# Attention phase: the row transform, the weights and the inverse joined in one product with four matrices of the image

## The chip, the cores and the metric

The program runs on one core of a Trainium2 chip. The metric is device time in microseconds (us). The five engines are TensorE (PE; its weight loads are shown as PEld), VectorE (DVE), ScalarE (ACT), GpSimd (POOL) and SyncE (SP, which issues DMAs). PSUM is the memory into which TensorE writes its products; SBUF is the on-chip memory for everything else.

## The reference, cut to what matters

Thirty-two images of 256 x 256. A three-level Haar transform splits each into a low band and three times three detail bands. Each band is multiplied by a weight of the image (a sigmoid for the low band, three softmaxes for the details, of dot products over the whole image), and the inverse transform gives the rows back. A class row is put in front, then come a causal attention with a residual, and a layer of eight experts.

```python
for _ in range(3):
    cur, h, v, d = _dwt2(cur)             # Haar split of columns and rows
    details.append((h, v, d))
aw = sigmoid(cur.reshape(B, -1) @ Wa + ba)
rec = cur * aw[:, :, None]
for (h, v, d), (Wd, bd) in zip(reversed(details), det_params):
    w = softmax(stack([h, v, d]).reshape(B, -1) @ Wd + bd)
    rec = _idwt2(rec, h * w[:, 0], v * w[:, 1], d * w[:, 2])
h = concatenate([cls_tok, rec], axis=1)   # 257 rows of 256 per image
e = _layernorm(h)
h = h + softmax(e @ R @ e.T + causal) @ e
h = h + ffn(_layernorm(h))                # top-k rows of each of 8 experts
```

## The kernel before, in words

One image is two tiles (h = 0, 1) of 128 rows by 256 columns. The kernel has a start (the band weights are turned into an image, and 64 products give the logits of 16 images; the second half follows between the first steps), the attention phase, a search for each expert's threshold, and the expert phase.

The attention phase is a software pipeline with an order written out by hand. Every engine runs the same list of steps t = 0 to 35: steps 0 to 7 stand one by one, 8 to 27 are a hardware loop of five iterations with four steps each, the rest stand one by one again. In step t each engine works on five images: a = t, b = t-1, c = t-2, d = t-3, m = t-4. Semaphores carry the waits between engines; within an engine the order of the code holds. Of an image:

- GpSimd, one step ahead (`columns`, L457 to L464): the column transform into `Xc` by sums and differences in three levels, two instructions each.
- TensorE (a, L854): the row transform, `fwd` x `Xc`, 512 output columns into bank `Zb`.
- VectorE (a): `Zb` times the table `W8` (L1279, two instructions), then the inverse column transform in three levels (L1284 to L1297) into `Q`.
- TensorE (b, L839): the inverse row transform `inv` x `Q` into bank `Hb`.
- VectorE (b): mean and variance of `Hb` (L1258, L1264). ScalarE (b): a copy of `Hb` into `hc` (L650).
- GpSimd (`emit`, L487 to L497): reciprocal deviations by a power (L492) and the scales that follow, for both layer norms at once: of b (input of attention) and of m (its output). It waits for the statistics of both. Behind them come `columns` of the next image and small copies into tables (L500, L472, L478).
- ScalarE (b, L663): the normalised rows `Ex`. TensorE (c, L847): their transpose; ScalarE (L641) copies it to `ET`. TensorE (c, L874): the product with R, 1024 columns; ScalarE (L656) copies it to `GT`. TensorE (c, L894, L896): the scores with the causal mask. VectorE (c, L1321, L1325): gate terms and row maxima.
- ScalarE (d, L634, L636): the exponentials. TensorE (d, L866): their transposes; ScalarE (L646) copies them. TensorE (d, L884 to L886): times the rows. VectorE (d): `U` (L1306), `H1` with the residual (L1314), its statistics (L1331, L1337). ScalarE writes `Yp` (m, L671) and `Bs` (one image older, L614), and SyncE stores both.

TensorE's order in a step is L839 (b), L847 (c), L854 (a), L866 (d), L874 (c), L884 to L886 (d), L894 and L896 (c). VectorE's is the first statistics (b), the inverse transform (a), `U` and `H1` (d), maxima (c), second statistics (d). ScalarE's is exponentials (d), `ET` (c), copy of transposes (d), `hc` (b), `Bs`, `GT` (c), `Ex` (b), `Yp` (m).

## Time and profile before

| what | value |
|---|---|
| median of 3 runs (lowest, highest) | 832.46 us (831.77, 833.66) |
| the profiled execution, its own time | 832.74 us |
| its span in the profile | 829.2 us |
| busy share of the span: PE, DVE, ACT, POOL | 89%, 70%, 55%, 56% |
| start, up to the first `fwd` product | 0 to 46.8 us |
| attention phase, up to the last `Bs` | about 46.8 to 329.6 us |
| threshold search, placing, first gathers | about 330 to 399 us |
| expert phase | about 399 to 829 us |

The page gives the busy time of each engine, the span in 40 slices, the DMA queues and the chain of work that ended last. Its busy shares are means over four phases with different limits, so the attention phase has to be read from windows and timelines of its own. In the rows below, a start time is that of the first of the instructions merged into the row (x2 is two instructions), the second number is their time from first start to last end, and a bracket at the end is the engine's idle time before them with what released it.

### The profile page before, as it was taken

How to read it: one execution, taken by the hardware profiler on the slowest of the kernel's cores; microseconds unless marked ns; L12 is line 12 of the kernel's file. 1: busy time of each engine (PE TensorE's matmuls, PEld its weight loads, DVE VectorE, ACT ScalarE, POOL GpSimd, SP SyncE). 2: the span in 40 equal slices, each digit the busy share in tenths (PEclk: the TensorE clock that was granted, in tenths of full speed). 3: DMA queues.
4: the chain of work that ended last, by engine and by line, in shares of the span. 5: the costliest groups of instructions: out<-in, count | busy, mean ns of one | idle time of the engine just before them, and what ended most of it. 6: DMA issues, size and time to landing. Idle time of an engine off the chain costs nothing.

```text
span 829.2 us, 15989 instructions
## 1 busy us (share of the span) xinstructions
PE 742.1 (89%) x4566; PEld 640.6 (77%) x4566; DVE 577.6 (70%) x1968; ACT 454.2 (55%) x1001; POOL 464.9 (56%) x744
## 2 busy tenths in 40 slices
PE   6988999999999984872799999999989999999994
PEld 3976667667667663761699998999989989999994
DVE  3765888888888876998878476684765856644431
ACT  1012677777777775200556665556655666566551
POOL 0155677777677755403426648467484673855533
PEclk9989999999999998555899999999999999999997
DMA  9900022122122122701213424334243352433222
GB/s 268 292 3 2 30 77 77 51 76 76 51 76 74 54 77 96 158 21 40 71 26 75 113 41 128 69 69 122 40 121 67 52 146 39 103 84 54 40 24 27
DMA packets 63570, 64.43 MB, mean 78 GB/s; under 512 B 14033, under 2 KB 57105, under 8 KB 63377
## 3 DMA queue, kind: packets, MB, share of 16 engines
q1 hardware_dynamic: 50576, 46.57, 18.7%
q0 software_dynamic: 12800, 17.12, 12.8%
q8 instruction: 26, 0.43, 0.2%
q14 instruction: 40, 0.32, 0.1%
q10 hardware_dynamic: 128, 0.00, 0.0%
HBM read 38.14 MB, written 25.53 MB: 77 GB/s over the span
## 4 chain that ended last, share of the span: by engine, by line
PE 33%; DVE 9%; issue 8%; POOL 5%; ACT 3%; DMA 2%; POOLq 0%; ACTq 0%; DVEq 0%; SPq 0%
PE bank L959 14%; PE bank L973 14%; PE bank L948 2%; DMA raw<-in_fc1T 2%; POOL w2l L517 2%; PE bank L985 1%; POOL out L553 1%; POOL yg L531 1%; ACT bank L706 1%; DVE Tc L1389 1%; DVE yl L1508 1%; DVE jk L1485 1%; PE bank L938 1%; DVE TR L1373 1%; DMA yg<-rows,idx 1%
## 5 line engine op out<-in xcount | busy, mean ns | idle before, releaser
L553 POOL DMA_INDIRECT out<-ob,sidx x72 | 114.0, 1583 | 159.4 <-ACT ob L722 145.7
L1515 DVE TENSOR_TENSOR hl<-bank,hh 128x384 fp32r<-128x384 f32 (+1 forms) x192 | 97.5, 513 | 138.5 <-ACT hh L709 134.8
L706 ACT ACTIVATE bank<-bank,b1s 128x384 f32<-128x384 f32 (+1 forms) x192 | 99.5, 518 | 137.7 <-PE bank L959 132.5
L959 PE MATMUL bank<-yh,w1h 128*128 128x384 f32 (+1 forms) x384 | 132.6, 345 | 9.5 <-DVE hl L1515 6.4
L959 PE MATMUL bank<-yh,w1l 128*128 128x384 f32 (+1 forms) x384 | 123.4, 321 | 0.0
L959 PE MATMUL bank<-yl,w1h 128*128 128x384 f32 (+1 forms) x384 | 122.9, 320 | 0.0
L973 PE MATMUL bank<-w2l,hh 128*128 128x256 f32 x384 | 108.0, 281 | 0.0
L973 PE MATMUL bank<-w2h,hh 128*128 128x256 f32 x384 | 108.0, 281 | 0.0
L973 PE MATMUL bank<-w2h,hl 128*128 128x256 f32 x384 | 107.9, 281 | 0.0
L531 POOL DMA_INDIRECT yg<-rows,idx x72 | 72.4, 1006 | 55.7 <-issue 50.6
L709 ACT ACTIVATE hh<-bank 128x384 fp32r<-128x384 f32 (+1 forms) x192 | 87.7, 457 | 6.1
L959 PEld LDWEIGHTS bank<-yh,w1h 128*128 128x128 f32 x384 | 73.8, 192 | 14.6 <-DVE hl L1515 7.8
L959 PEld LDWEIGHTS bank<-yl,w1h 128*128 128x128 f32 x384 | 73.5, 191 | 0.0
L959 PEld LDWEIGHTS bank<-yh,w1l 128*128 128x128 f32 x384 | 72.8, 190 | 0.0
L973 PEld LDWEIGHTS bank<-w2l,hh 128*128 128x128 f32 x384 | 72.6, 189 | 0.0
L973 PEld LDWEIGHTS bank<-w2h,hh 128*128 128x128 f32 x384 | 72.5, 189 | 0.0
L973 PEld LDWEIGHTS bank<-w2h,hl 128*128 128x128 f32 x384 | 72.5, 189 | 0.0
L874 PE MATMUL bank<-ET,Rw 128*128 128x256 f32 x256 | 62.4, 386 | 0.0
L874 PEld LDWEIGHTS bank<-ET,Rw 128*128 128x128 f32 x256 | 46.0, 189 | 9.7 <-issue 3.3
L894 PE MATMUL bank<-GT,ET 128*128 128x137 f32 (+1 forms) x256 | 52.5, 340 | 0.7 <-ACT GT L656 0.7
L492 POOL TENSOR_TENSOR ST<-A,mhalf 128x6 f32<-128x6 f32 x36 | 50.7, 1408 | 3.0
L663 ACT ACTIVATE ARENA<-bank,N,ST 128x256 f32<-128x256 f32 x64 | 32.6, 560 | 33.0 <-POOL O L497 33.0
(224 smaller groups left out, 1815.5 us busy)
## 6 DMA issues: line engine op xcount, KB each, us to landing
BIG<-in_x SPq DMA_DIRECT2D x4, 2048.0 KB, 16.4
out<-Bs SPq DMA_DIRECT2D x32, 256.0 KB, 2.2
rows<-Yp SPq DMA_DIRECT2D x32, 256.0 KB, 2.4
raw<-in_fc1T SPq DMA_DIRECT2D x16, 512.0 KB
raw<-in_fc2T SPq DMA_DIRECT2D x16, 512.0 KB
yg<-rows,idx POOLq DMA_INDIRECT x72, 2.9
out<-ob,sidx POOLq DMA_INDIRECT x72, 3.8
gwb<-in_gate_w SPq DMA_DIRECT2D x1, 1024.0 KB, 7.2
```

What stands on the lines that cost most here:

```text
L492: g.tensor_tensor(st[:, 8:14], A6[:, :], mhalf[:, :], ALU.pow).then_inc(s["pow"], 1)
L517: rest = g.tensor_tensor(flat(lo, half), raw[:, half * NF:(half + 1) * NF], flat(hi, half), ALU.subtract)
L531: g.indirect_dma_start(out=yg[eh][0:m, t, :], out_offset=None, in_=rows, in_offset=tok(ap=idx[eh][0:m, t:t + 1], axis=0))\
L553: g.indirect_dma_start(out=out_rows, out_offset=tok(ap=sidx[job.eh][0:m, t:t + 1], axis=0), in_=ob[t % 3][0:m, :], in_offset=None, compute ...
L663: last = A.activation(Ex[b.r][:, h, 0:D], Hb[:, h * D:(h + 1) * D], ACT.Identity, bias=N6[t.p][:, h:h + 1], scale=ST[t.p][:, 8 + h:9 + h])
L706: A.activation(h[:, 0:cur.w], h[:, 0:cur.w], ACT.Gelu_apprx_tanh, bias=b1s[:, bass.ds(cur.e, 1), f]).then_inc(s["hact"], 1)
L709: A.activation(hT[cur.p][0][:, f, 0:cur.w], h[:, 0:cur.w], ACT.Copy).then_inc(s["hhi"], 1)
L874: last = T.matmul(Rb[:, e * D:(e + 1) * D], Rw[:, j, e * P:(e + 1) * P], ET[c.p][:, j, 1:NT], start=(j == 0), stop=(j == 1))
L894: T.matmul(Sb[:, c0:c0 + w], ET[c.p][:, j, 1 + h * P:1 + (h + 1) * P], GT[c.p][:, j, 0:w], start=(j == 0), stop=False)
L959: last = T.matmul(Lb[ring(cur, f)][:, 0:cur.w], w1s[cur.eh][i][:, d, f * P:(f + 1) * P], yT[cur.p][k][:, d, 0:cur.w], start=(n == 0), stop ...
L973: mm = T.matmul(bank[4 + t % 2][:, 0:D], hT[prev.p][i][:, f, at:at + P], w2s[prev.eh][k][:, f, :], start=(n == 0), stop=(n == 23))
L1515: v.tensor_tensor(hT[cur.p][1][:, f, 0:cur.w], Lb[ring(cur, f)][:, 0:cur.w], hT[cur.p][0][:, f, 0:cur.w], ALU.subtract).then_inc(s["hlo"], 1)
```

## The change

The row transform, the multiplication by the weights and the inverse row transform of an image are all linear maps on its 128 rows, and a Haar transform of three levels mixes only rows within blocks of 8. So for each of the four column bands (`LEAF` = 4) there is one matrix `inv` x diag(weights) x `fwd`, with the same 8 x 8 block sixteen times on its diagonal. The change builds these blocks once per half of the images into a table `OB` (128 x 32 images x 32): VectorE expands the weights (`mix_blocks`), TensorE folds them with one product of 512 columns (`fold`), ScalarE copies the product to `OB` (`mix_table`). In each step GpSimd spreads the blocks of the next image into the four 128 x 128 matrices `OP` (`operators`: one multiplication by a mask, 512 elements per partition). TensorE makes four products with them in place of the two before, 640 output columns in place of 1024. The column transform stops at two levels: the pair for the third (L463, L464) goes, and the last product reads its columns in exchanged pairs instead.

VectorE no longer multiplies by the table. It copies the low band (128 elements) and makes the last two levels of the inverse column transform straight from PSUM into `hc`, then takes the first statistics from `hc`, all for image a in step t and not for b. ScalarE's copy into `hc` goes, and `Ex` is made from `hc`. TensorE's and ScalarE's other instructions keep their order. In step 3 TensorE waits for the logits' mask and not for the table.

```diff
-for _name, _n in [("ident", P), ("fwd", P), ("inv", P), ("same", P), ("before", P), ("causal", P),
-                  ("sign", 3), ("slot", 9), ("batch", 1), ("diag", CG), ("pick", NJ), ("spread", 4 * P),
+for _name, _n in [("ident", P), ("same", P), ("before", P), ("causal", P),
+                  ("sign", 3), ("slot", 9), ("batch", 1), ("diag", CG), ("pick", NJ), ("fold", P), ("mixed", 4 * CG), ("blocks", P),
                   ("owner", 5), ("rep1", P), ("rep2", P), ("rep3", 2 * P), ("halves", 2 * BITS)]:
...
-                po.wait_ge(s["xc_l"], m.n * 2 + 1)
-                g.tensor_tensor(L2[:, :, :], L1[:, :, 0::2], L1[:, :, 1::2], ALU.add).then_inc(s["xc_l"], 1)
-                g.tensor_tensor(dst[:, :, 64:128], L1[:, :, 0::2], L1[:, :, 1::2], ALU.subtract)
-                po.wait_ge(s["xc_l"], m.n * 2 + 2)
-                g.tensor_tensor(dst[:, :, 0:32], L2[:, :, 0::2], L2[:, :, 1::2], ALU.add)
-                g.tensor_tensor(dst[:, :, 32:64], L2[:, :, 0::2], L2[:, :, 1::2], ALU.subtract).then_inc(s["xc"], 1)
+                po.wait_ge(s["xc_l"], m.n + 1)
+                g.tensor_tensor(dst[:, :, 0:64], L1[:, :, 0::2], L1[:, :, 1::2], ALU.add)
+                g.tensor_tensor(dst[:, :, 64:128], L1[:, :, 0::2], L1[:, :, 1::2], ALU.subtract).then_inc(s["xc"], 1)
+
+            def operators(m):
+
+                after(po, "z_done", m.n - 1)
+                apart(po)
+                blocks = OB[:, bass.ds(m.n, 1), :].rearrange("p b (g k) -> p (b g) k", g=LEAF)
+                g.tensor_tensor(OP[m.p].rearrange("p g (r k) -> p g r k", k=CG),
+                                blocks.unsqueeze(2).to_broadcast([P, LEAF, P // CG, CG]),
+                                cst("blocks").rearrange("p (r k) -> p r k", k=CG).unsqueeze(1)
+                                .to_broadcast([P, LEAF, P // CG, CG]), ALU.mult).then_inc(s["wide"], 1)
...
                     columns(nxt)
+                    if isinstance(t.n, int) and t.n == HEAD - 1:
+                        po.wait_ge(s["w8"], 2)
+                    operators(nxt)
...
             columns(Step(0, 0))
+            po.wait_ge(s["w8"], 1)
+            operators(Step(0, 0))
...
+            def mix_table(i):
+
+                act.wait_ge(s["w8_mm"], i + 1)
+                A.activation(OB[:, i * HB:(i + 1) * HB, :].rearrange("p b k -> p (b k)"), ZP[:, :], ACT.Copy)\
+                    .then_inc(s["w8"], 1)
+            mix_table(0)
...
-                if b:
-                    after(act, "h1", b.n - 3)
-                    act.wait_ge(s["st0_b"], b.n + 1)
-                    A.activation(hc[b.r][:, :, :], Hb[:, :].rearrange("p (h c) -> p h c", h=NH), ACT.Copy)
...
-                        last = A.activation(Ex[b.r][:, h, 0:D], Hb[:, h * D:(h + 1) * D], ACT.Identity,
+                        last = A.activation(Ex[b.r][:, h, 0:D], hc[b.r][:, h, :], ACT.Identity,
...
+                T.matmul(ZP[:, :], cst("fold")[0:CG * NJ, :], bw8[:, :, :].rearrange("p b k -> p (b k)"),
+                         start=True, stop=True).then_inc(s["w8_mm"], 1)
...
-                    after(pe, "hcE", b.n)
-                    pe.wait_ge(s["q"], b.n + 1)
-                    T.matmul(Hb[:, :], cst("inv"), Q[b.p].rearrange("p h c -> p (h c)"), start=True, stop=True)\
-                        .then_inc(s["h0"], 1)
...
-                    after(pe, "zw", a.n * 2)
+                    after(pe, "q", a.n)
+                    pe.wait_ge(s["wide"], a.n + 1)
                     pe.wait_ge(s["xc"], a.n + 1)
-                    T.matmul(Zb[:, :], cst("fwd"), Xc[a.p].rearrange("p h c -> p (h c)"), start=True, stop=True)\
-                        .then_inc(s["z_done"], 1)
+                    X, Z = Xc[a.p], Zb[:, :].rearrange("p (h c) -> p h c", h=NH)
+                    T.matmul(Z[:, :, 128:256], OP[a.p][:, 3, :], X[:, :, 128:256], start=True, stop=True)
+                    T.matmul(Z[:, :, 64:128], OP[a.p][:, 2, :], X[:, :, 64:128], start=True, stop=True)
+
+                    T.matmul(Z[:, :, 0:64], OP[a.p][:, 0, :], X[:, :, 0:64], start=True, stop=False)
+                    T.matmul(Z[:, :, 0:64].rearrange("p h (c s) -> p h c s", s=2), OP[a.p][:, 1, :],
+                             X[:, :, 0:64].rearrange("p h (c s) -> p h c s", s=2)[:, :, :, ::-1],
+                             start=False, stop=True).then_inc(s["z_done"], 1)
...
-                    pe.wait_ge(s["w8"], 2)
+                    pe.wait_ge(s["lg_m"], 2)
...
+            def mix_blocks(i):
 
                 dve.wait_ge(s["z_mm"], 2 * i + 2)
-                v.tensor_copy(bwT[:, i * HB:(i + 1) * HB], ZP[i][0:NJ, 32:32 + HB]).then_inc(s["bw_c"], 1)
-
-            def mix_table(i):
-
-                dve.wait_ge(s["w8_mm"], i + 1)
-                for q, (c0, c1) in enumerate(((0, 1), (1, 2), (2, 4), (4, 8))):
-                    last = v.tensor_copy(W8[:, i * HB:(i + 1) * HB, c0:c1],
-                                         ZP[i][:, 128 + q * HB:128 + (q + 1) * HB].unsqueeze(2)
-                                         .to_broadcast([P, HB, c1 - c0]))
-                last.then_inc(s["w8"], 1)
+                after(dve, "w8_mm", i)
+                v.tensor_tensor(bw8[:, :, :], ZP[0:CG * NJ, 32:32 + HB].unsqueeze(2).to_broadcast([CG * NJ, HB, LEAF * CG]),
+                                cst("mixed")[0:CG * NJ, :].unsqueeze(1).to_broadcast([CG * NJ, HB, LEAF * CG]), ALU.mult)\
+                    .then_inc(s["bw_c"], 1)
...
+                if a:
+
+                    dve.wait_ge(s["z_done"], a.n + 1)
+                    Z = Zb[:, :].rearrange("p (h c) -> p h c", h=NH)
+                    v.tensor_copy(I2[:, :, :], Z[:, :, 0:64]).then_inc(s["i4"], 1)
+                    dve.wait_ge(s["i4"], a.n + 1)
+                    v.tensor_tensor(I1[:, :, 0::2], I2[:, :, :], Z[:, :, 64:128], ALU.add)
+                    v.tensor_tensor(I1[:, :, 1::2], I2[:, :, :], Z[:, :, 64:128], ALU.subtract).then_inc(s["inv"], 1)
+                    dve.wait_ge(s["inv"], a.n + 1)
+                    v.tensor_tensor(hc[a.r][:, :, 0::2], I1[:, :, :], Z[:, :, 128:256], ALU.add)
+                    v.tensor_tensor(hc[a.r][:, :, 1::2], I1[:, :, :], Z[:, :, 128:256], ALU.subtract).then_inc(s["q"], 1)
+                    dve.wait_ge(s["q"], a.n + 1)
                     for h in range(NH):
-                        last = v.bn_stats(bn0[:, h, :], Hb[:, h * D:(h + 1) * D])
+                        last = v.bn_stats(bn0[:, h, :], hc[a.r][:, h, :])
                     last.then_inc(s["st0_b"], 1)
-                if b:
-                    dve.wait_ge(s["st0_b"], b.n + 1)
+
+                    after(dve, "tab", t.n)
+                    dve.wait_ge(s["st0_b"], a.n + 1)
                     apart(dve)
                     for h in range(NH):
-                        last = v.bn_aggr(st[:, 2 * h:2 + 2 * h], bn0[:, h, :])
+                        last = v.bn_aggr(ST[1 - t.p][:, 2 * h:2 + 2 * h], bn0[:, h, :])
...
-                    for g0, g1 in ((0, 2), (2, 8)):
-                        w = W8[:, bass.ds(a.n, 1), g0:g1].to_broadcast([P, NH, g1 - g0]).unsqueeze(3)\
-                            .to_broadcast([P, NH, g1 - g0, 32])
-                        v.tensor_tensor(Zw.rearrange("p h (g c) -> p h g c", g=8)[:, :, g0:g1, :],
-                                        Zb[:, :].rearrange("p (h g c) -> p h g c", h=NH, g=8)[:, :, g0:g1, :], w,
-                                        ALU.mult).then_inc(s["zw"], 1)
-                    dve.wait_ge(s["zw"], a.n * 2 + 1)
-                    lo, hi = Zw[:, :, 0:32], Zw[:, :, 32:64]
-                    v.tensor_tensor(I2[:, :, 0::2], lo, hi, ALU.add)
-                    v.tensor_tensor(I2[:, :, 1::2], lo, hi, ALU.subtract).then_inc(s["inv"], 1)
-                    dve.wait_ge(s["zw"], a.n * 2 + 2)
-                    dve.wait_ge(s["inv"], a.n * 2 + 1)
-                    hi = Zw[:, :, 64:128]
-                    v.tensor_tensor(I1[:, :, 0::2], I2[:, :, :], hi, ALU.add)
-                    v.tensor_tensor(I1[:, :, 1::2], I2[:, :, :], hi, ALU.subtract).then_inc(s["inv"], 1)
-
-                if a:
-                    dve.wait_ge(s["inv"], a.n * 2 + 2)
-                    after(dve, "h0", a.n - 1)
-                    hi = Zw[:, :, 128:256]
-                    v.tensor_tensor(Q[a.p][:, :, 0::2], I1[:, :, :], hi, ALU.add)
-                    v.tensor_tensor(Q[a.p][:, :, 1::2], I1[:, :, :], hi, ALU.subtract).then_inc(s["q"], 1)
...
+            row = haar[p, 0:CG]
+            mixed[j, :, g, :] += (1 / 8, 1 / 8, 1 / 4, 1 / 2)[g] * scale[p] * np.outer(row, row)
+    mixed[:, :, 0, :], mixed[:, :, 1, :] = mixed[:, :, 0, :] + mixed[:, :, 1, :], mixed[:, :, 0, :] - mixed[:, :, 1, :]
+    put("mixed", mixed.reshape(NJ * CG, LEAF * CG))
+    put("fold", m[:, None] % CG == q[None, :] % CG)
+    put("blocks", q[:, None] // CG == q[None, :] // CG)
```

GpSimd, step 7, the last one ahead of the loop, from the scales of the step to the table copy. Before (`Xc` and `L1` lie in ARENA, the image in BIG):

```order
L495 TENSOR_TENSOR N<-ST,nm 128x4
L496 TENSOR_TENSOR N<-ST,nm 128x2
L497 TENSOR_SCALAR O<-ST 128x2
L457 TENSOR_TENSOR ARENA<-BIG 128x256
L458 TENSOR_TENSOR ARENA<-BIG 128x2x128
L460 TENSOR_TENSOR ARENA<-ARENA 128x128
L461 TENSOR_TENSOR ARENA<-ARENA 128x2x64
L463 TENSOR_TENSOR ARENA<-ARENA 128x2x32
L464 TENSOR_TENSOR ARENA<-ARENA 128x2x32
L500 COPY TST<-ST 128x16
```

GpSimd at the same place now (`OP` lies in ARENA too, the mask in C):

```order
L503 TENSOR_TENSOR N<-ST,nm 128x4
L504 TENSOR_TENSOR N<-ST,nm 128x2
L505 TENSOR_SCALAR O<-ST 128x2
L458 TENSOR_TENSOR ARENA<-BIG 128x256
L459 TENSOR_TENSOR ARENA<-BIG 128x2x128
L461 TENSOR_TENSOR ARENA<-ARENA 128x2x64
L462 TENSOR_TENSOR ARENA<-ARENA 128x2x64
L469 TENSOR_TENSOR ARENA<-OB,C 128x512
L511 COPY TST<-ST 128x16
```

The pair with 64 outputs is gone, and one instruction with 512 stands in its place, ahead of the table copy.

VectorE, step 7, from the first statistics to `U`. Before:

```order
L1258 BN_STATS bn<-bank 128x6 x2
L1264 BN_AGGR ST<-bn 128x2 x2
L1272 RECIPROCAL ST<-rsm 128x2
L1279 TENSOR_TENSOR ARENA<-bank,W 128x2x64
L1279 TENSOR_TENSOR ARENA<-bank,W 128x2x192
L1284 TENSOR_TENSOR ARENA<-ARENA 128x64
L1285 TENSOR_TENSOR ARENA<-ARENA 128x64
L1289 TENSOR_TENSOR ARENA<-ARENA 128x128
L1290 TENSOR_TENSOR ARENA<-ARENA 128x128
L1296 TENSOR_TENSOR ARENA<-ARENA 128x256
L1297 TENSOR_TENSOR ARENA<-ARENA 128x256
L1306 SCALAR_TENSOR_TENSOR ARENA<-CX,ARENA,bank 128x264 x2
```

VectorE at the same place now:

```order
L1283 COPY ARENA<-bank 128x128
L1285 TENSOR_TENSOR ARENA<-ARENA,bank 128x128
L1286 TENSOR_TENSOR ARENA<-ARENA,bank 128x128
L1288 TENSOR_TENSOR hc<-ARENA,bank 128x256
L1289 TENSOR_TENSOR hc<-ARENA,bank 128x256
L1292 BN_STATS bn<-hc 128x6 x2
L1299 BN_AGGR ST<-bn 128x2 x2
L1305 RECIPROCAL ST<-rsm 128x2
L1313 SCALAR_TENSOR_TENSOR ARENA<-CX,ARENA,bank 128x264 x2
```

The first statistics moved behind the inverse transform, and they are now those of the step's own image.

TensorE, step 7, from the inverse to the product with R (Rw). Before:

```order
L839 MATMUL bank<-ARENA,C 128x512
L847 MATMUL bank<-C,ARENA 128x128 x4
L854 MATMUL bank<-ARENA,C 128x512
L866 MATMUL bank<-C,ARENA 128x128 x3
L874 MATMUL bank<-ET,Rw 128x256 x4
```

TensorE at the same place now:

```order
L870 MATMUL bank<-C,ARENA 128x128 x4
L879 MATMUL bank<-ARENA 128x2x128
L880 MATMUL bank<-ARENA 128x2x64
L882 MATMUL bank<-ARENA 128x2x64
L883 MATMUL bank<-ARENA 128x2x64
L896 MATMUL bank<-C,ARENA 128x128 x3
L855 MATMUL bank<-ET,Rw 128x256 x4
```

The inverse (L839) is gone, so the transposes of c come first, and four products stand where `fwd` stood.

## Rows read from the trace of the kernel before

**Rows 1.** Windows: busy us (instructions) of each engine, granted TensorE clock, DMA share, GB/s.
```profile
200.00:300.00 100.00, 98.06 (x451) 69.33 (x449) 87.38 (x310) 74.77 (x179) 73.28 (x207) 1.00 0.19 65
```

**Rows 2.** Timeline of one step: start us, us, engine, line, tiles, [idle <-releaser].
```profile
202.63 1.97 PE L874 MATMUL bank<-ET,Rw 128*128 128x256 f32 x8
...
204.43 0.61 PE L884 MATMUL bank<-ARENA 128*128 128x264 f32 x2
...
205.97 0.89 DVE L1306 SCALAR_TENSOR_TENSOR ARENA<-CX,ARENA,bank 128x264 f32<-128x264 f32 x2 [0.47 <-PE bank L886]
...
206.95 1.03 DVE L1314 SCALAR_TENSOR_TENSOR H<-ARENA,ST,hc 128x256 f32<-128x256 f32 x2
...
207.99 0.61 DVE L1325 TENSOR_REDUCE nmx<-bank 128x1 f32<-128x129 f32 x2
...
208.64 0.37 ACT L634 ACTIVATE ARENA<-bank,nmx 128x129 f32<-128x129 f32 x1 [0.58 <-DVE nmx L1325]
...
209.36 0.25 DVE L1337 BATCH_NORM_AGGREGATE ST<-bn 128x2 f32<-128x6 f32 x2
209.44 0.60 ACT L641 ACTIVATE ET<-bank 128x512 f32<-128x512 f32 x1
...
210.19 1.97 PE L874 MATMUL bank<-ET,Rw 128*128 128x256 f32 x8
```

**Rows 3.** Timelines: key product early and late, one stall, two H1 updates.
```profile
90.88 0.30 PEld L839 LDWEIGHTS bank<-ARENA,C 128*128 128x128 f32 x2 [1.68 <-ACT ARENA L663]
...
93.90 1.90 PE L874 MATMUL bank<-ET,Rw 128*128 128x256 f32 x8
...
292.79 1.26 DVE L1314 SCALAR_TENSOR_TENSOR H<-ARENA,ST,hc 128x256 f32<-128x256 f32 x2
...
300.65 0.88 DVE L1314 SCALAR_TENSOR_TENSOR H<-ARENA,ST,hc 128x256 f32<-128x256 f32 x2
...
303.81 1.97 PE L874 MATMUL bank<-ET,Rw 128*128 128x256 f32 x8
...
311.30 1.97 PE L874 MATMUL bank<-ET,Rw 128*128 128x256 f32 x8
```

**Rows 4.** Timeline of the same step: GpSimd and the first product.
```profile
202.72 0.25 DVE L1264 BATCH_NORM_AGGREGATE ST<-bn 128x2 f32<-128x6 f32 x2
...
203.12 0.22 POOL L487 TENSOR_SCALAR A<-ST 128x4 f32<-128x4 f32 x1 [1.60 <-DVE ST L1264]
...
204.73 0.43 DVE L1296 TENSOR_TENSOR ARENA<-ARENA 128x256 f32<-128x256 f32 x1
...
205.98 0.61 POOL L457 TENSOR_TENSOR ARENA<-BIG 128x256 f32 x1
...
208.21 0.29 POOL L463 TENSOR_TENSOR ARENA<-ARENA 128x64 f32<-128x64 f32 x1
...
208.80 1.13 PE L854 MATMUL bank<-ARENA,C 128*128 128x512 f32 x2
```

**Rows 5.** Timeline at the end of one loop iteration.
```profile
178.79 0.76 DVE L1258 BATCH_NORM_STATS2 bn<-bank 128x6 f32<-128x256 f32 x2 [0.36 <-issue]
...
184.21 1.12 PE L839 MATMUL bank<-ARENA,C 128*128 128x512 f32 x2 [0.38 <-ACT ARENA L663]
```

**Rows 6.** Groups of instructions by form, GpSimd: x count | busy us, mean ns | idle.
```profile
L517 POOL TENSOR_TENSOR w2l<-raw,w2h 128x1024 fp32r<-128x1024 f32 x16 | 38.4, 2401 | 5.2 <-ACT w2h L685 4.9
...
L460 POOL TENSOR_TENSOR ARENA<-ARENA 128x128 f32<-128x128 f32 x32 | 17.3, 540 | 0.0
```

**Rows 7.** DMA issues of the start: KB each, us to landing.
```profile
C<-in_const SPq DMA_DIRECT2D x1, 940.0 KB, 4.9
```

**Rows 8.** Timeline of the start and the first steps.
```profile
7.68 15.41 PE L759 MATMUL bank<-ARENA,C 64*128 64x384 f32 x40 [7.68 <-DMA ARENA<-in_Wd]
...
46.78 2.05 PE L854 MATMUL bank<-ARENA,C 128*128 128x512 f32 x2
...
61.45 1.10 PE L854 MATMUL bank<-ARENA,C 128*128 128x512 f32 x2
```

103 lines of the change are left out of this document (50 added, 53 removed).

## The prediction

> **What bounds the kernel now.** I read the windows first, since the page's shares are means over four phases and the change touches the start and the attention phase alone. In the attention phase TensorE is busy 98.06 us of 100, VectorE 87.38, ScalarE 74.77, GpSimd 73.28, at full clock [rows 1]. That invites the reading that TensorE sets the pace and that every column taken from it comes back as time. The timelines say otherwise, so I followed one step by its starts.
>
> The attention chain of a step [rows 2]: the product with R starts at 202.63; 1.80 us later the products of the probabilities (204.43); 1.54 later `U` (205.97), for which VectorE had sat idle 0.47; 0.98 to `H1` (206.95); 1.04 to the maxima (207.99); 0.65 to the exponentials (208.64), before which ScalarE was idle 0.58; 0.80 to the copy `ET` (209.44), which stands behind the exponentials in ScalarE's order; 0.75 to the next product with R (210.19). Sum 7.56 us, the whole step. The chain closes on itself: each R product stands ahead of the next image's probabilities on TensorE, and the next `ET` behind that image's exponentials on ScalarE. The change touches no link of it. A better witness is at the end of the phase: from 303.81 to 311.30 [rows 3] the loop has run out of images, there is no first product, no inverse, no column transform and no weights, and the step still takes 7.49 us.
>
> A second chain runs through GpSimd and takes two steps [rows 4]. First statistics end at 202.97 (202.72 + 0.25), GpSimd starts 0.15 later, 2.86 later (205.98) it begins the columns, and the first product starts when they are done, at 208.80; then 1.39 to the R product of rows 2.
>
> A third shows at the loop's end [rows 5]: VectorE takes the first statistics 0.36 us late at 178.79, and the inverse product, which needs the `Ex` made from them, starts at 184.21 after an idle 0.38 with ScalarE's `Ex` as releaser. Between the R starts at 93.90 and 303.81 [rows 3] lie 27 steps in 209.91 us, 7.774 each, against 7.56 for the good one: such late steps make the mean.
>
> **The change part by part.**
>
> *TensorE.* 1024 columns become 640. R's 1024 columns take 1.80 us [rows 2], 1.76 ns each, so 384 fewer are 0.68 us per step, off a busy time of 98.06% of 7.774, or 7.62. TensorE falls to about 6.95. By the chain of rows 2 this is worth nothing directly: R starts when `ET` is there. What it buys is slack ahead of R. The inverse goes with its wait for `Ex`; the transposes take that wait over.
>
> *VectorE.* In place of eight instructions on SBUF and the table, and of statistics from PSUM, there are a copy, four sums and the same statistics. None of the five has more outputs than the 256 of L1296, 0.43 us [rows 4], though one operand now lies in PSUM: at most 2.15. Statistics of this kind and their join took from the maxima's end (207.99 + 0.61) to 209.61, 1.0 us [rows 2]. The first products will end some 1.35 us after their start; the start was 208.80, so 210.15, and `U` is due at 205.97 + 7.56 = 213.53. At most 3.15 us of work fits into the 3.38 between them. So nothing of it shows, with 0.2 to 0.8 of slack; if the sums from PSUM took 0.55 each, `U` would be 0.4 late in every step. The statistics are now ready a step ahead of GpSimd's need.
>
> *ScalarE.* The copy of `Hb` goes, about 0.6 us like the `ET` copy of the same size [rows 2]. It was behind the exponentials and `ET`, so it is off the chain and worth nothing.
>
> *GpSimd.* It loses the pair from 208.21 to the product's start at 208.80, 0.59 us [rows 4], and gains one multiplication of 512 elements. No row of before has these operands (two inputs, one repeated over rows, the other over matrices). The nearest in length is the subtraction of 1024 in 2401 ns, 2.34 ns each [rows 6]: 1.20 us. The dearest is L460 at 540 ns for 128 outputs, 4.22 ns each [rows 6]: 2.16 us. The cheapest is L457 at 0.61 for 256 [rows 4], no less. I take 1.20, with 0.10 for the start and the hand-over, because the added one reads and writes in runs of eight neighbours while L460 reads every second element. Bounds: 1.1 and 2.3.
>
> Now the two-step chain with the new wait (`wide`), which every image's first product has. GpSimd starts when the second statistics end, at 209.61 in rows 2, and no longer after the first ones. Hand-over 0.15; to the columns 2.86; four column instructions 2.23 (205.98 to 208.21); multiplication 1.30; first products and transposes 1.39 plus 128 columns more, 0.22: 1.61; R to probabilities 1.80; to `U` 1.54; `U` to the end of the second statistics 3.64 (205.97 to 209.61). Sum 15.13 for two steps, 7.57 each. Behind the waiting product on TensorE stand the transposes of the probabilities, R and all else, so a late GpSimd would delay the whole step. GpSimd's own load: 73.28% of 7.774 is 5.70, minus 0.59 plus 1.30, 6.41 us: it fits.
>
> The Trainium skill ("GPSIMD Engine Reference", Performance versus the Vector engine) puts two-input elementwise work at about 2.6 cycles of 1.2 GHz per element. By it the multiplication would take an estimated 1.11 us and the chain 7.53 a step; the row's 2.34 ns is a little above, so the sum stays with the row.
>
> So both chains ask for 7.56 to 7.57. The late steps should mostly go: the 0.36 of VectorE at the loop's end falls into its slack, and `Ex` comes 0.9 us earlier, since GpSimd starts after the second statistics (209.61, a step earlier 202.05) and no longer after the first (202.97). I leave 0.1 for each of the five ends, which makes 7.6 a step with the jitter of rows 2, and 0.5 beside it. Gain: 209.91 - 27 x 7.6 = 4.7, less 0.5: 4.2.
>
> *The start.* The constants shrink from 1880 to 1400 columns, 940 to 700 KB. Their DMA took 4.9 us [rows 7], and the first products wait at 7.68 for a transfer behind it on the same queue [rows 8]. 240/940 of 4.9 is 1.25, an upper bound since part of it is latency; I take 0.8 earlier, for all that follows. Against that, the first product of image 0 (46.78) now waits for the table: a product of 512 columns in place of eight small ones, ScalarE's copy (0.6) in place of VectorE's, and GpSimd's multiplication (1.3). The last two are 1.9 us, of which I take half as covered by the class row's products; 128 columns more cost 0.5 there, where 512 took 2.05 and not the 1.10 of the same product at 61.45 [rows 8]. That is 1.5 later. In step 5 the inverse's weights sat 1.68 us waiting for `Ex` [rows 3]; that wait goes with GpSimd's earlier start, and I take 1.2 of it. Net 0.5 earlier; bounds 2.0 earlier (0.8 + 1.2, the table's path all covered) and 2.0 later (1.9 + 0.5 and nothing gained in step 5, less 0.4 for the constants).
>
> *After the phase* nothing is changed; the last steps without first products keep their 7.49.
>
> Sum against the profiled execution: 832.74 - 4.2 - 0.5 = 828.0. The median shown is 832.46, 0.28 below that execution; a difference this small is below what can be told, so 828.0 stands.
>
> **The rivals.**
>
> *B, GpSimd becomes the bound (slower).* If the multiplication takes L460's 4.22 ns per element, its term is 2.26 instead of 1.30, the two-step chain 16.09, 8.05 a step. 27 x (8.05 - 7.774) = 7.5 more, and the start some 0.5 later instead of earlier: 840.7. It decides from a chain of 15.55, that is, from a multiplication of about 1.7 us. For it: twelve instructions of GpSimd now stand between the second statistics and the first product, and the sum has no slack. Against: L457 and the 1024-element row both say 2.3 to 2.4 ns, the former with reads of every second element as well.
>
> *C, `H1` is slowed in each step.* The two `H1` instructions take 1.26 us beside column instructions, 1.03 in the good step, 0.88 beside nothing [rows 2, 3]. They lie on the attention chain. Now GpSimd works from 3.0 to 6.5 us after the second statistics on columns and multiplication, and `H1` starts 4.9 after them (206.95 + 7.56 - 209.61). If the multiplication slows both halves like the worst columns do, the chain is 7.56 + 0.23 = 7.79 or, from 7.49 + 0.38, 7.87; I take 7.83. 27 x 0.06 = 1.5 more, less 0.5: 833.7. The Trainium skill ("GPSIMD Engine Reference", Key points) says that GpSimd contends for its SBUF interfaces with VectorE instructions that have two SBUF inputs. `H1` is such a one, and the three durations agree. By that rule the second half of `H1` would be slowed by the multiplication, as the first is by the last column instruction.
>
> *D, the long steps stay.* They come from the branch itself and not from the statistics' way to `Ex`. Then the step keeps 7.774 and only the start counts: 832.2. Against it: the releaser in rows 5 is `Ex`.
>
> *E, more comes back.* If `H1` falls between GpSimd's instructions that do no harm, the attention chain is 7.49: 27 x 0.284 = 7.7 and 0.5 from the start: 824.5.
>
> **How the numbers follow.** Forecast 0.50 (825.5 to 830.7, from a multiplication of 1.1 to 1.4 and the start's bounds), B 0.15, C 0.15, D 0.10, E 0.10. The range 824.0 to 834.5 leaves out B and about a twentieth more, the far ends of E and C. This kernel's measurement tells 0.2% from no change, 1.7 us, so faster means below 830.8 and slower above 834.1. Faster: 0.48 of the forecast, E 0.10, C 0.04, D 0.02, 0.64. Same: C 0.08, D 0.07, 0.02 of the forecast, 0.17. Slower: B 0.15, C 0.03, D 0.01, 0.19.
>
> **What would show it.** The R product's starts should lie 7.5 to 7.65 apart, without a long one at each loop's end; TensorE should be idle some 0.5 us a step ahead of the R product or the transposes, released by ScalarE, and its busy share of the window should fall to about 91%; VectorE should still wait for the probabilities ahead of `U`. The multiplication's mean should be 1.15 to 1.35. The first products of TensorE should start at 7.68 - 0.8, and the gap between R's starts at the step numbers of 93.90 and 303.81 should be near 205.7. I am wrong if the first product waits for the multiplication by more than 0.3 us in most steps (B), if `H1` is 1.2 us or more throughout (C), or if VectorE starts `U` later than the probabilities allow because its new sums run late.

## The result: slower by 3.4%

The changed kernel takes 860.68 us (median of 4 runs, 858.98 to 862.99) against 832.12 us (4 runs, 831.29 to 833.66): ratio 1.034, 95% interval 1.0318 to 1.0362. Forecast were 828.0 us and a range of 824.0 to 834.5. The profiled execution took 860.9 us, its span 859.1; before these were 832.74 and 829.2.

Where the 29.9 us of span lie, by the starts of four instructions:

| from, to | before | after | difference |
|---|---|---|---|
| start to the R product of the step at 93.90 [rows 3] | 93.90 | 95.15 | +1.25 |
| 27 steps from there | 209.91 (7.774 each) | 229.93 (8.516 each) | +20.02 |
| from there to the first placing product | 76.18 | 77.48 | +1.30 |
| from there to the end | 449.21 | 456.54 | +7.33 |

The attention phase again, windows of the changed kernel, columns as in [rows 1]. TensorE's busy share fell to 83 where 91 was forecast, and every other engine but GpSimd fell too: a new wait, not new work.

```profile
200.00:300.00 100.00, 82.89 (x457) 67.90 (x456) 80.51 (x244) 64.05 (x153) 73.93 (x175) 1.00 0.18 63
```

The attention chain of one step, to be laid beside [rows 2]: timeline of the changed kernel (start us, us, engine, line, tiles, idle and releaser).

```profile
202.09 1.96 DVE L1321 SCALAR_TENSOR_TENSOR H<-ARENA,ST,hc 128x256 f32<-128x256 f32 x2
202.09 1.27 POOL L469 TENSOR_TENSOR ARENA<-OB,C 128x512 f32<-128x512 f32 x1
...
203.42 0.70 PE L879 MATMUL bank<-ARENA 128*128 128x256 f32 x2 [0.38 <-POOL ARENA L469]
203.97 0.16 DVE L1328 COPY ARENA<-bank 128x16 f32<-128x16 f32 x1
204.05 0.61 DVE L1332 TENSOR_REDUCE nmx<-bank 128x1 f32<-128x129 f32 x2
...
204.77 0.37 ACT L655 ACTIVATE ARENA<-bank,nmx 128x129 f32<-128x129 f32 x1 [2.39 <-DVE nmx L1332]
...
205.58 0.59 ACT L663 ACTIVATE ET<-bank 128x512 f32<-128x512 f32 x1
...
205.83 0.52 PE L896 MATMUL bank<-C,ARENA 128*128 128x128 f32 x3 [1.05 <-ACT ARENA L657]
...
206.32 1.97 PE L855 MATMUL bank<-ET,Rw 128*128 128x256 f32 x8
...
208.13 0.61 PE L911 MATMUL bank<-ARENA 128*128 128x264 f32 x2
...
209.66 0.89 DVE L1313 SCALAR_TENSOR_TENSOR ARENA<-CX,ARENA,bank 128x264 f32<-128x264 f32 x2 [1.33 <-PE bank L913]
```

`H1` (L1321) and GpSimd's multiplication (L469) start in the same hundredth of a microsecond, and `H1` takes 1.96 us for 1.03 [rows 2] or 0.88 [rows 3]. All links behind it keep their lengths to 0.07 us; ScalarE waits 2.39 us for the maxima (0.58 before). One step is 8.55 us, 7.49 + 1.06, and this repeats in each step that has a multiplication. The multiplication starts 6.6 us after the end of the previous `H1` (204.05 to 210.64), by way of the second statistics. `H1` starts, by way of the exponentials, after just as long (the next one stands at 210.64 too), and so they meet again.

The expert part lost 7.3 us, though its code is unchanged. TensorE's waits there, by releaser (us in total, times, longest), in the changed kernel; the kernel before has no wait for issue at this line:

```profile
PE bank L986 <- issue: 8.0, 2, 4.0
```

They lie at 628 to 637 us, where the expert loop's first pass (experts 1 and 5) ends and the program jumps back for the second. The windows there, columns as above, show 16 us with TensorE half busy (8.0 us), and the granted clock at its lower level (0.50, 1.2 GHz) behind the idle time:

```profile
628.00:632.00 4.00, 0.61 (x6) 0.40 (x4) 3.82 (x9) 1.23 (x3) 3.70 (x3) 0.84 0.48 73
632.00:636.00 4.00, 0.68 (x1) 0.50 (x2) 1.70 (x3) 0.00 (x0) 3.67 (x3) 0.50 0.74 187
636.00:640.00 4.00, 2.71 (x11) 2.70 (x11) 0.00 (x0) 0.73 (x2) 3.14 (x3) 0.50 0.44 124
640.00:644.00 4.00, 4.00 (x27) 4.00 (x27) 1.04 (x2) 1.88 (x4) 0.00 (x0) 0.88 0.29 100
```

The queue that brings instructions moved more, too. Its row in the list of DMA queues (packets, MB, share), before and then after:

```profile
q8 instruction: 26, 0.43, 0.2%
```
```profile
q8 instruction: 36, 0.59, 0.3%
```

### The profile page after: what moved, and what is told of

It reads as the page before. It is cut to its first block, busy times and chain, and to the rows that moved or that the text cites. A ratio compares the mean times of both kernels' runs of the same rounds, so it can differ in the third digit from the quotient of the medians.

```text
span 859.1 us, 15856 instructions
## 1 busy us (share of the span) xinstructions
PE 728.0 (85%) x4684; PEld 655.1 (76%) x4684; DVE 578.3 (67%) x1870; ACT 443.3 (52%) x971; POOL 483.6 (56%) x712
## 4 chain that ended last, share of the span: by engine, by line
PE 32%; DVE 9%; issue 8%; POOL 5%; ACT 3%; DMA 2%; POOLq 0%; ACTq 0%; DVEq 0%; SPq 0%
PE bank L986 14%; PE bank L1000 13%; PE bank L1012 2%; PE bank L975 2%; POOL out L566 2%; POOL w2l L530 2%; POOL yg L544 1%; DMA raw<-in_fc1T 1%; ACT bank L727 1%; DVE Tc L1396 1%; DVE yl L1515 1%; DVE jk L1492 1%; PE bank L965 1%; DVE TR L1380 1%; DVE ohu L1467 1%
## 5 line engine op out<-in xcount | busy, mean ns | idle before, releaser
L1321 DVE SCALAR_TENSOR_TENSOR H<-ARENA,ST,hc 128x256 f32<-128x256 f32 x64 | 57.6, 938 | 2.8
L1313 DVE SCALAR_TENSOR_TENSOR ARENA<-CX,ARENA,bank 128x264 f32<-128x264 f32 x64 | 28.4, 485 | 42.6 <-PE bank L913 42.6
```

What stands on the lines that cost most here:

```text
L1313: last = v.scalar_tensor_tensor(out=U[d.p][:, h, :], in0=CX[:, :], scalar=Pr[d.p][:, 129 * h:129 * h + 1], in1=Ab[h][:, 0:DG], op0=ALU.mul ...
L1321: last = v.scalar_tensor_tensor(out=H1[d.p][:, h, :], in0=U[d.p][:, h, 0:D], scalar=st_next[:, 14 + h:15 + h], in1=hc[d.r][:, h, :], op0=A ...
```

## The experiments

Two causes were in question: who holds `H1`, and what stalls the expert loop. Ratios are to the kernel before the change, run on the same chip.

### What holds H1

**The multiplication moved.** In `emit` of GpSimd, from behind `columns` to behind the two table copies, with its wait for the second half of the table:

```
+                if nxt:
+                    if isinstance(t.n, int) and t.n == HEAD - 1:
+                        po.wait_ge(s["w8"], 2)
+                    operators(nxt)
                 if b:
                     after(po, "hcE", b.n - 1)
...
                 if nxt:
                     columns(nxt)
-                    if isinstance(t.n, int) and t.n == HEAD - 1:
-                        po.wait_ge(s["w8"], 2)
-                    operators(nxt)
```

> GpSimd's multiplication (128x512, 1.27 us) is issued 2 us later in the program: behind its two table copies of the next step and ahead of its statistics, where it has idled 1.2 us for combine1's result in the changed kernel. Nothing is left out. Theory (a GpSimd instruction that is running when H1 is ready holds H1 until it ends, and nothing else went wrong): H1 meets at most the last column instruction (0.40 us), so it takes 0.9 to 1.3 us for 1.95, the statistics start up to 0.3 us later, the distance from one R product to the next falls from 8.55 to 7.5 to 7.9 us, and the kernel takes 860.7 - 31 x (0.65 to 1.05) = 828 to 841 us. Rival 1 (the product of each image is late because the multiplication ends late: TensorE waited 0.37 us per step for it): gains at most 0.37 x 31 = 11 us, 849, and H1 stays at 1.95. Rival 2 (VectorE's five sums that read PSUM are what lengthened the step): nothing changes, 861.

Measured 832.32 us, ratio 0.9998 (0.9988 to 1.0008): 28 us came back by moving one instruction. The timeline of one step:

```profile
202.99 0.89 DVE L1314 SCALAR_TENSOR_TENSOR ARENA<-CX,ARENA,bank 128x264 f32<-128x264 f32 x2 [1.32 <-PE bank L914]
...
203.74 0.40 POOL L462 TENSOR_TENSOR ARENA<-ARENA 128x128 f32<-128x128 f32 x1
203.96 0.88 DVE L1322 SCALAR_TENSOR_TENSOR H<-ARENA,ST,hc 128x256 f32<-128x256 f32 x2
204.09 0.42 POOL L512 COPY TST<-ST 128x16 f32 x1
204.76 0.17 DVE L1329 COPY ARENA<-bank 128x16 f32<-128x16 f32 x1
...
205.58 1.27 POOL L469 TENSOR_TENSOR ARENA<-OB,C 128x512 f32<-128x512 f32 x1
```

The multiplication still takes 1.27 us, but `H1` 0.88 (0.88 to 1.03 in the attention loop); the R products lie 7.4 to 7.6 us apart. Rivals 1 and 2 are out: the wait of 0.38 for L469 couldn't give 28 us, and the sums from PSUM are unchanged. The expert part kept its loss: the first placing product is at 375.87 us (379.99 before), the span 832.3 (829.2).

**Half of the multiplication.** `gs = slice(0, 2)` for the matrices from the third image on; the other two matrices keep old values.

> From the third step on GpSimd's multiplication makes two of the four matrices (256 elements in each partition for 512); the other two keep what an earlier step left in them, so this leaves out half of the weights' work. Place and count of the instruction are the changed kernel's. Theory (held for the rest of the running instruction): the multiplication takes 0.65 us for 1.27 and H1 1.30 to 1.40 for 1.95; the step is 8.55 - 0.6 = 7.95 us and the kernel 860.7 - 30 x 0.6 = 843 us. Rival (contention as two streams sharing a rate): H1 overlaps only 0.65 us of traffic at half speed, so it takes 0.88 + 0.33 = 1.2 us, the step 7.8 and the kernel 838. Rival (the sums that read PSUM): 861.

Measured 845.71 us, ratio 1.0162 (1.0134 to 1.0191).

**A copy in its place.** It leaves out the mask.

```
-                g.tensor_tensor(OP[m.p]..., blocks..., cst("blocks")..., ALU.mult)
+                g.tensor_copy(OP[m.p].rearrange("p g (r k) -> p g r k", k=CG),
+                              blocks.unsqueeze(2).to_broadcast([P, LEAF, P // CG, CG]))
```

> The multiplication is a copy of the same 512 elements at the same place: one input, the table of blocks repeated over the columns; the mask is left out, so the matrices aren't block-diagonal. Theory in its narrow form (only two two-input instructions from SBUF shut each other out): H1 is back at 0.88 us, the step at 7.5 and the kernel at 860.7 - 31 x 1.05 = 828 us. Theory in its wide form (any GpSimd instruction holds H1 while it runs): a copy of 512 elements takes at least 0.4 us, so H1 takes 0.88 plus the copy's duration and the step 7.49 plus it. The duration of H1 beside the copy tells the two apart. Rival (the sums that read PSUM): 861.

Measured 841.56 us, ratio 1.0092 (1.0064 to 1.012). The narrow form is out: an instruction with one input holds `H1` as well.

**H1 with one input in PSUM.** `in1=Ab[h][:, 0:D]` for `in1=hc[d.r][:, h, :]`, and TensorE's `after(pe, "u", d.n)` becomes `after(pe, "h1", d.n)`. It leaves out the residual.

> H1's second input is the product in PSUM (128x256 of the bank that U has just read) for hc in SBUF, so H1 reads one input from SBUF and one from PSUM; the residual is left out of H1. TensorE's AV of the next step waits for H1 for U, which comes 0.9 us earlier and is not late. GpSimd is as in the changed kernel. Theory (H1 is held because both its inputs are in SBUF): H1 takes 0.9 us though the multiplication of 1.27 us runs beside it, the step is 7.5 us and the kernel 860.7 - 31 x 1.05 = 828 us. Rival (any VectorE instruction is held beside a GpSimd multiplication, or GpSimd slows what reads PSUM too): H1 stays at 1.95 us and the kernel at 861.

Measured 830.77 us, ratio 0.9986 (0.997 to 1.0001), with 7.47 us a step and the expert part's stall still in it (36 packets). The multiplication and `H1` again run side by side, and neither minds:

```profile
209.09 0.87 DVE L1321 SCALAR_TENSOR_TENSOR H<-ARENA,ST,bank 128x256 f32<-128x256 f32 x2
209.17 1.27 POOL L469 TENSOR_TENSOR ARENA<-OB,C 128x512 f32<-128x512 f32 x1
209.88 0.17 DVE L1328 COPY ARENA<-bank 128x16 f32<-128x16 f32 x1
```

Laid side by side, with the distance from `U`'s start to the start of the gate copy behind `H1` (1.77 us when nothing holds it) as the measure:

| GpSimd's instruction beside H1 | its time | U to copy | delay |
|---|---|---|---|
| multiplication of 512 (changed kernel, 209.66 to 212.52) | 1.27 | 2.86 | 1.09 |
| multiplication of 256 (208.05 to 210.36) | 0.73 | 2.31 | 0.54 |
| copy of 512 (207.38 to 209.55) | 0.61 | 2.17 | 0.40 |
| none (moved, 202.99 to 204.76) | – | 1.77 | 0 |
| multiplication of 512, H1 with PSUM input (208.11 to 209.88) | 1.27 | 1.77 | 0 |

The delay is the GpSimd instruction's time less 0.2 us in all three holds, whatever the number of elements: `H1` waits for the instruction's end. Two streams that share a rate would have given 1.2 us for `H1` beside the half; it took 1.41 (209.03).

This does not hold for every GpSimd instruction. In each step of the kernel before, the power (L492) runs beside four sums of VectorE with two SBUF inputs (L1289 to L1297), and between 90 and 310 us these take 0.28 to 0.43 us in every step and are never held. It reads two inputs of only 6 elements per partition; what sets it apart from the multiplication was not tested.

```profile
203.98 1.35 POOL L492 TENSOR_TENSOR ST<-A,mhalf 128x6 f32<-128x6 f32 x1
...
205.07 0.42 DVE L1297 TENSOR_TENSOR ARENA<-ARENA 128x256 f32<-128x256 f32 x1
```

**Four short multiplications**, one for each matrix, in a loop over `LEAF`.

> The changed kernel with GpSimd's multiplication as four instructions of 128 elements, one for each of the four matrices, at the same place. Nothing is left out. The multiplications take 4 x 0.35 to 0.4 = 1.4 to 1.6 us together. Theory A (H1 waits for the GpSimd instruction that is running and then has its turn): H1 is held for one piece ahead of each of its halves at most, so it takes 0.88 + 0.3 to 0.7 = 1.2 to 1.6 us for 1.95, and the kernel 860.7 - 31 x (0.35 to 0.75) = 837 to 850 us. Theory B (GpSimd keeps what they share as long as it has instructions ready): H1 takes 0.88 + 1.4 to 1.6 = 2.2 us or more, and the kernel 861 to 875.

Measured 843.85 us, ratio 1.012 (1.0101 to 1.014), theory A:

```profile
203.63 0.89 DVE L1314 SCALAR_TENSOR_TENSOR ARENA<-CX,ARENA,bank 128x264 f32<-128x264 f32 x2 [0.67 <-PE bank L914]
204.61 1.34 DVE L1322 SCALAR_TENSOR_TENSOR H<-ARENA,ST,hc 128x256 f32<-128x256 f32 x2
205.88 0.16 DVE L1329 COPY ARENA<-bank 128x16 f32<-128x16 f32 x1
```

The four take 2.06 us and `H1` 1.34. Taken apart, the four take 0.46, 0.64, 0.63 and 0.45 us and the halves of `H1` 0.75 and 0.67: the first of the four goes ahead of the first half of `H1`, the second waits for that half, and so on. The two engines take turns, an instruction each.

**The multiplication first in the next step**, ahead of the table copies.

> The multiplication stands first in GpSimd's next step: behind the copy of the step's statistics and ahead of the two table copies, so that it is ready while H1 runs. Nothing is left out. H1 ends its first half about when the copy of the statistics ends. Theory A (an H1 that is running is not broken, but GpSimd may have its turn between H1's two halves): the multiplication starts between the halves and holds the second one for 1.27 us, H1 takes 1.9 to 2.1 us, and the kernel 855 to 861. If instead both halves of H1 go first, the multiplication ends 1.3 us behind H1, the statistics don't wait for it, H1 takes 0.9 us and the kernel is at 832 us like the kernel with the multiplication behind the copies, or up to 2 us faster.

Measured 859.53 us, ratio 1.0318 (1.029 to 1.0346), theory A again:

```profile
210.47 0.20 POOL L512 COPY TST<-ST 128x16 f32 x1
210.49 1.90 DVE L1322 SCALAR_TENSOR_TENSOR H<-ARENA,ST,hc 128x256 f32<-128x256 f32 x2
210.62 1.49 POOL L469 TENSOR_TENSOR ARENA<-OB,C 128x512 f32<-128x512 f32 x1
```

The multiplication, held for some 0.2 us itself (mean 1.47 for 1.27), slips in between the halves and holds the second.

**The kernel before, with H1 reading PSUM.** The edit of the fourth experiment, without the change.

> The kernel before the change, with H1's second input from the product in PSUM for hc in SBUF; the residual is left out of H1. Theory (whatever GpSimd runs holds an H1 with two SBUF inputs): H1 took 1.15 us for each image in the 28 steps from 93.9 to 311.3 us (56 halves busy 32.2 us) for 0.88 alone, so H1 takes 0.88 in all, the step falls from 7.76 to 7.5 us, the 8.15 us steps at the loop's ends go, and the kernel takes 832.9 - 28 x 0.27 = 825.4 us, 824 to 827. Rival (the two-step chain through GpSimd's columns bounds the step at 7.56, and the loop's end is paid for by instruction issue): the long steps stay, 829 to 833.

Measured 825.65 us, ratio 0.9919 (0.9903 to 0.9935). `H1` takes 0.87 to 0.89 us. Most steps are 7.39 to 7.48 us; of those at the loop's ends five are 7.76 to 7.86 for 8.11 to 8.22 and one 7.55 for 8.02. So the kernel before paid 0.27 us a step, 7 us in all, to the same hold, by its short column instructions. The long steps, expected to go, went only in part: some 0.3 us of each is not the hold's.

### What stalls the expert loop

**90 instructions more in TensorE's program**, on top of the moved multiplication:

```
+            for _ in range(180):
+                pe.wait_ge(s["ld_const"], 16)
             pe.wait_ge(s["vsp_t"], 2)
```

> The kernel with the multiplication moved, and 90 instructions more in TensorE's program: 180 waits on a semaphore that has long been reached, two to an instruction, ahead of its wait for the last gates, where it idles over 5 us. Nothing is left out. What it is for: the kernel with the multiplication moved reached the expert part 4.1 us before the kernel before did (first placing product at 375.9 us, 380.0 us before) and still ended 3.1 us later, and 6.3 us of that is TensorE idle for 'issue' at 602 to 610 us, where the expert loop's first pass ends and TensorE's program jumps back (8.0 us in the changed kernel, none in the kernel before). The changed program's loop of 1607 TensorE instructions begins 94 instructions later than before. Theory (the jump back is served from instructions already fetched or not, by where the loop lies in the program): another 90 instructions move it to where the jump is served again, the 6.3 us go, and the kernel takes 832.3 - 6 to 7.5 = 825 to 826.5 us. Rival (the stall has to do with when the pass ends, or with what the other engines fetch then): it stays, 832. Cost of the added waits if they are not hidden: some 2 us. By the Trainium skill's page 'Runtime: NRT & Kernel Launch', section 'Instruction fetch mechanics', instructions come in blocks of 256 and a jump out of the blocks held must fetch first; no trace here shows the size of a block.

Measured 827.16 us, ratio 0.9927 (0.9912 to 0.9942). No wait for issue is left there, and the instruction queue has 27 packets. The first placing product is at 374.73 us and the rest takes 450.0 us, as before (449.2).

**The changed kernel with the same 90.**

> The changed kernel, with the multiplication where it is, and 90 instructions more in TensorE's program ahead of the wait for the last gates. Nothing is left out. Theory (two causes that add up: H1 held for 1.07 us in each step, and the stall of 8.0 us at the expert loop's jump back): the stall goes and the steps stay at 8.55 us, so 860.7 - 5 to 8 = 853 to 856 us. Rival (the stall is gone in the padded kernel only because its expert part began earlier): 861.

Measured 855.44 us, ratio 1.0291 (1.0267 to 1.0315), 27 packets. The two causes add up: 5 us for the stall here, the rest for `H1`.

**The kernel before with 110, 70 and 94 instructions more** (`range(220)`, `range(140)`, `range(188)`).

> The kernel before the change, with 110 instructions more in TensorE's program at the same place (220 waits on a semaphore that has long been reached, two to an instruction). The change itself is not in it. The expert loop then begins 110 instructions later than in the kernel before, as it began 94 later in the changed kernel. Theory (where the loop lies decides whether the jump back stalls): TensorE idles 4 to 8 us at the end of the loop's first pass and the kernel takes 832.5 + 5 to 8 = 838 to 840.5 us. Rival (the stall came with the change's own work, or with its timing): no stall, 832.5, or up to 2 us more where the added waits aren't hidden.

> The kernel before the change, with 70 instructions more in TensorE's program at the place of the earlier padding (140 waits on a semaphore long reached, two to an instruction); 110 gave no stall. Theory: the jump back at the end of the expert loop's first pass is served without a fetch as long as the loop touches few enough blocks of instructions, which depends on where it begins. The loop has 1607 instructions. Counted from the first one of the program, the loop begins at 3679 before, 3773 in the changed kernel (stall), 3789 (before with 110 more, none), 3863 (multiplication moved and 90 more, none). With blocks of 256 instructions (the Trainium skill, 'Runtime: NRT & Kernel Launch', section 'Instruction fetch mechanics') the loop touches 7 or 8 of them, 8 where its first one lies past the 185th of a block; the four results fit if some 51 to 66 instructions stand ahead of those counted, and then 3749 (this kernel) lies in the stalling stretch. Expected: instruction packets on queue 8 at 36 for 26, TensorE idle for 'issue' by 2 to 8 us near 605 to 615 us, the kernel at 834.5 + 2 to 7 = 836 to 842 us. Rival (the stall belongs to the change's own work and has nothing to do with the place): 26 or 27 packets, no idle, 833 to 834.5.

> The kernel before the change, with 94 instructions more in TensorE's program (188 waits on a semaphore long reached), so that its expert loop begins at the 3773rd instruction, where the changed kernel's does. Theory 1 (the place alone decides): 36 packets on the instruction queue for 26, TensorE idle for 'issue' 2 to 8 us at the loop's jump back, 836 to 842 us. Theory 2 (the place decides together with something else that the change moved, such as where the attention loop lies, or the padding's instructions don't count as one each in what is fetched): 26 or 27 packets, no stall, 832.5 to 834.5 us.

Measured: 110 more, 834.5 us, ratio 1.0009 (0.9996 to 1.0021), 27 packets; 70 more, 832.93 us (12 runs, 828.93 to 838.21), 1.001 (0.9988 to 1.0032), 27 packets in the profiled execution; 94 more, 838.85 us, 1.0097 (1.006 to 1.0134), 36 packets. My first two guesses of the place missed, and the third, which copied the changed kernel's place exactly, brought the loss into a kernel without the change. Its windows:

```profile
604.00:608.00 4.00, 2.99 (x23) 2.46 (x21) 3.73 (x17) 1.59 (x5) 2.96 (x4) 1.00 0.51 83
608.00:612.00 4.00, 0.68 (x1) 0.50 (x2) 3.49 (x4) 0.49 (x2) 3.83 (x2) 0.60 0.35 89
612.00:616.00 4.00, 2.76 (x11) 2.75 (x11) 0.34 (x1) 0.78 (x2) 3.51 (x4) 0.50 0.63 159
```

**The moved multiplication with 16 and 40 instructions more** (`range(32)`, `range(80)`).

> The kernel with the multiplication moved, and 16 instructions more in TensorE's program (32 waits), so that the expert loop begins at the 3789th, a place that gave no stall in the kernel before the change. Theory 1 (the place alone decides): no stall, 827 us. Theory 2: 36 packets and a stall, 832 us.

> As the run before, with 40 instructions more (80 waits), the loop at the 3813th. With 90 more there was no stall, with none there was. Theory 1: no stall, 827 us. Theory 2 (a stretch of places wider than 16): 36 packets and a stall if the stretch reaches beyond 40, and then 832 us; otherwise 827.

Measured 826.28 us, ratio 0.9933 (0.9907 to 0.9958), and 826.57 us, ratio 0.9938 (0.9921 to 0.9954), 27 packets each. Both beat both kernels, as the one with 90 does; the three can't be told apart.

All kernels in one table, by the number of the expert loop's first instruction in TensorE's program:

| first instruction | kernels | packets on the instruction queue |
|---|---|---|
| 3679 | before, and with the PSUM input | 26 |
| 3749 | before + 70 | 27 (one execution of 829.51 us) |
| 3773 | changed, moved, half, copy, PSUM input, split, front, before + 94 | 36 in all eight |
| 3789 | before + 110, moved + 16 | 27 |
| 3813, 3863 | moved + 40; moved + 90, changed + 90 | 27 |

The loop's place alone decides: 94 instructions without the change bring the loss, and 16 more on top of the change, its multiplication moved, take it away. What is fetched can be read from the times of the packets. In the kernel before, the instruction queue has none during the loop's second pass (605.1 to 710.6 us), and none in the other kernels with 27 packets. In the changed kernel it has nine there (627.6 to 740.5 us), as in the kernel before with 94 more, and one more had come by the jump (21 for 20). These are the ten more: where the jump back stalls, the whole second pass is fetched again.

By the Trainium skill ("Runtime: NRT & Kernel Launch", Instruction fetch mechanics) TensorE has room for 2048 instructions, refilled in blocks of 256, and a taken branch out of the current two blocks has to fetch first. A packet here is 0.43 MB / 26 = 16.5 KB, or 64 bytes for each of 256 instructions, which agrees with the block. The two blocks don't agree: from 3679 or 3789 the jump goes back over 1607 instructions, more than six blocks, and no packet comes. An estimate from the page's sizes, that the jump stalls where the loop touches 8 blocks and not 7, gives a stretch of 70 starting places. The profiled executions make it narrower than 40, from above 3749 to below 3789. That is open at its lower end: of the twelve runs at 3749 three took 837.15 to 838.21 us, as long as those at 3773 (837.75 to 842.67), and the other nine 828.93 to 833.68. No trace of the three is kept, so a stall in some executions there is neither shown nor excluded.

## Why the prediction was wrong

Forecast was a span of 829.2 - 4.7 = 824.5; it is 859.1, 34.6 more: 24.2 in the 27 steps (229.93 for 205.7), 1.75 at the start, 8.6 after them.

- **The failed step, 24.2 us:** "7.6 a step with the jitter of rows 2". What the forecast called jitter, `H1` at 1.03 or 1.26 for 0.88, was the hold by GpSimd's column instructions. It named the mechanism as rival C and then mis-sized it: "if the multiplication slows both halves like the worst columns do", 0.38 us. Its sign for C, `H1` at 1.2 us or more throughout, is what came: 1.90 to 2.04 us. A hold lasts until the instruction that holds has ended. A column instruction of 0.61 us can hold for 0.4, the multiplication of 1.27 us for 1.09. The price should have been the new instruction's own length: at most 7.49 + 1.27 = 8.76 a step, and 7.49 + 1.09 = 8.58 with the delay measured; the step is 8.55. The Trainium skill's sentence on contention ("GPSIMD Engine Reference", Key points) is borne out for two SBUF inputs; that sentence has no price, and I took one from the wrong rows. The kernel before held a dearer one, with `H1` 0.80 us late behind two column instructions, one ahead of each half:

```profile
89.70 1.68 DVE L1314 SCALAR_TENSOR_TENSOR H<-ARENA,ST,hc 128x256 f32<-128x256 f32 x2
89.73 0.61 POOL L457 TENSOR_TENSOR ARENA<-BIG 128x256 f32<-128x256 f32 x1
90.30 0.79 POOL L458 TENSOR_TENSOR ARENA<-BIG 128x256 f32<-128x256 f32 x1
```

- **The meeting itself** could have been read: the text put GpSimd's work at 3.0 to 6.5 us after the second statistics, multiplication last, and `H1` at 4.9. By the sum's own terms the multiplication was to run from 5.2 to 6.5, on `H1`'s second half, and one late link is enough to meet both.
- **GpSimd:** right. The multiplication takes 1.27 us for the forecast 1.20 + 0.10, so B didn't happen. B's price came from a row that the hold itself had lengthened: L460, 540 ns on average, ran beside `H1`; the same sum in the changed kernel (L461), beside `U` with an input in PSUM, takes 0.40 us.
- **The late steps at the loop's ends:** right. No step of the changed kernel's loop stands out (8.46 to 8.64). More went than the hold: the 0.3 us that the kernel before kept at these steps with `H1` reading PSUM are gone too. The forecast put them down to VectorE's late statistics, which fits and was not tested by itself.
- **TensorE's columns worth nothing, VectorE's five sums within their slack:** right. With the multiplication moved the step is 7.49 us on average, and `U` waits for the probabilities (1.32 us in the row shown).
- **Start:** -0.5 forecast, +1.25 measured. The constants brought the first product from 7.68 to 7.17 us, 0.51 for the 0.8 taken. The first product of image 0 came at 47.51 (46.78 [rows 8]), R(0) 1.58 late (63.96 for 62.38) and R(2) 1.80 (86.51 for 84.71). The 1.2 us hoped for in step 5 came: from R(2) to R(3), which is the R product at 93.90, the kernel before took 9.19 us and the one with the multiplication moved 7.57; the changed kernel took 8.64, since the hold is paid there too. R(0) isn't steady, though: it stands at 62.59 to 65.56 us in the eleven traces with the change and at 59.67 to 62.90 in the five without it, so some of the 1.25 may be chance.
- **"After the phase nothing is changed":** wrong by 8.6 us, though no line there was. 7.3 us is the stall, which no view of the kernel before could show; that TensorE's program ahead of the loop grew could be seen. The other 1.3 us go with the last probabilities' products, at the lower clock: 1.09 us each (L912) for 0.61 before (L885).
- **The sign** was given 0.19, nearly all of it by B. Without both causes the change is a gain: 826.3 us (0.9933), near the 824.5 of rival E plus the late start.

## What to carry to other kernels

Before GpSimd gets a long instruction, look where VectorE has instructions with two SBUF inputs on the critical chain: price a meeting at the full length of GpSimd's instruction. Then place that instruction where VectorE works from PSUM or with one input, or give the VectorE instruction a PSUM input. Where a change moves a long loop in TensorE's program, compare the packets of the instruction queue between the two kernels; if they differ, shift the loop by a few instructions (16 were enough here) before judging the change.

## What the runs showed of the hardware

- `H1`, a VectorE instruction with two SBUF inputs, and a GpSimd instruction of 128 to 512 elements per partition shut each other out for whole instructions, and take turns; a GpSimd copy with one input does it as well (0.61 us, `H1` 0.40 later). With one input in PSUM `H1` is not held at all beside 1.27 us of GpSimd.
- Not every GpSimd instruction does this: the power of 6 elements (1.35 us) held none of four sums with two SBUF inputs.
- It works both ways: beside `H1`, GpSimd's multiplication takes 1.47 us for 1.27.
- A jump back in TensorE's program cost 5 to 7 us once, when the loop began at its 3773rd instruction, and nothing at 3679, 3789, 3813 or 3863, in kernels with and without the change; at 3749 the profiled execution had no stall. Where it stalled, the second pass of 1607 instructions was fetched again in nine packets; elsewhere none was.
